# A Flamingo layer on one core: the queries' rms factor moved from q into the exponential, and the transposes of k moved behind the first value matmuls

## What is computed

```
xn = layernorm(x)
q  = rms_norm(xn @ q_w.T + q_b, norm_q_w)          # one rms factor per token, over all 512 features
k  = rms_norm(ctx @ k_img_w.T + k_img_b, norm_k_img_w)
v  = ctx @ v_img_w.T + v_img_b
p  = softmax(q k^T / sqrt(32))                     # per head, 128 x 128
x  = x + tanh(g_xattn) * ((p v) @ o_w.T + o_b)
h  = square(relu(layernorm(x) @ up_w)) @ down_w + (layernorm(x) @ expert_weight) * (sum of the 2 largest gates)
x  = x + tanh(g_ffn) * (layernorm(h) * gamma + beta)
```

## Time and profile before

| | |
|---|---|
| median of 3 runs | 1550.09 us (1548.4 to 1550.29) |
| span of the profiled execution | 1548.3 us; its time outside the profile is not listed apart |
| PE busy | 1499.5 us, 97% of the span |
| VectorE, ScalarE, GpSimd busy | 58%, 45%, 29% |
| attention part | about the first 690 us |
| feed-forward part | the rest |

### The profile page before, as it was taken

The page is one execution under the profiler, slowest core; times in us unless marked ns, Lnnn a source line. Parts: engine busy times, 40 slices in busy tenths (PEclk is TensorE's granted clock), DMA queues, the critical chain, the costliest instruction groups (busy, mean ns, idle before and its releaser), DMA issues.

```text
span 1548.3 us, 22150 instructions
## 1 busy us (share of the span) xinstructions
PE 1499.5 (97%) x6912; PEld 1201.4 (78%) x6912; DVE 892.5 (58%) x1474; ACT 689.9 (45%) x1951; POOL 443.8 (29%) x582
## 2 busy tenths in 40 slices
PE   5999999999999999989999999999999999999996
PEld 4777777777777777767878878878788788788785
DVE  6877777777777777774634334353353343433524
ACT  5667677766676777664422222222222222222221
POOL 3455545444555454440002011020020120200202
PEclk9999999999999999999999999999999999999998
DMA  7222222222222222414310010010100100210100
GB/s 232 62 83 79 68 76 81 70 73 81 81 75 67 81 81 68 123 42 136 109 55 28 1 62 20 14 61 7 54 27 0 54 27 1 67 41 0 41 14 27
DMA packets 76353, 91.75 MB, mean 59 GB/s; under 512 B 7072, under 2 KB 39968, under 8 KB 76320
## 3 DMA queue, kind: packets, MB, share of 16 engines
q1 hardware_dynamic: 76320, 91.34, 19.3%
HBM read 57.76 MB, written 16.78 MB: 48 GB/s over the span
## 4 chain that ended last, share of the span: by engine, by line
PE 78%; DVE 10%; ACT 6%; issue 3%; POOL 1%; DMA 1%; SPq 1%; ACTq 0%; DVEq 0%; POOLq 0%
PE bank L73 14%; PE bank L75 14%; PE bank L74 14%; PE wide L73 10%; PE wide L74 10%; PE wide L75 10%; DVE kf L455 3%; PE bank L270 3%; DVE pT_lo L374 2%; DVE qf L479 2%; ACT pT_hi L537 2%; ACT junk_q L602 1%; ACT junk_k L585 1%; PE bank L824 1%; PE bank L290 1%
## 5 line engine op out<-in xcount | busy, mean ns | idle before, releaser
L1082 ACT ACTIVATE relu<-bank 128x512 f32<-128x512 f32 x128 | 76.7, 599 | 423.6 <-PE bank L75 423.6
L1120 DVE TENSOR_TENSOR hid<-relu 128x512 f32<-128x512 f32 x128 | 97.1, 759 | 269.5 <-ACT relu L1082 269.4
L558 ACT ACTIVATE prob<-wide,nmx 128x128 f32<-128x128 f32 x512 | 180.6, 403 | 39.3 <-DVE nmx L401 39.3
L73 PE MATMUL wide<-down_hi,hT_hi 128*128 128x512 f32 x384 | 152.2, 396 | 0.0
L75 PE MATMUL bank<-wk_hi,up_lo 128*128 128x512 f32 x384 | 152.0, 396 | 0.0
L74 PE MATMUL wide<-down_lo,hT_hi 128*128 128x512 f32 x384 | 151.6, 395 | 0.0
L74 PE MATMUL bank<-wk_lo,up_hi 128*128 128x512 f32 x384 | 151.6, 395 | 0.0
L73 PE MATMUL bank<-wk_hi,up_hi 128*128 128x512 f32 x384 | 151.6, 395 | 0.0
L75 PE MATMUL wide<-down_hi,hT_lo 128*128 128x512 f32 x384 | 151.5, 394 | 0.0
L1122 DVE TENSOR_TENSOR hT_lo<-hid,hT_hi 128x512 fp32r<-128x512 f32 x128 | 89.6, 700 | 89.8 <-ACT hT_hi L1071 89.8
L670 POOL TENSOR_TENSOR prob<-prob,rr 128x512 f32<-128x512 f32 x128 | 137.8, 1087 | 0.0
(11 more groups left out here) (156 smaller groups left out, 3624.7 us busy)
## 6 DMA issues: line engine op xcount, KB each, us to landing
kd<-kT SPq DMA_DIRECT2D x128, 128.0 KB, 2.4
xin<-in_x SPq DMA_DIRECT2D x32, 256.0 KB, 2.7
cin<-in_ctxT SPq DMA_DIRECT2D x32, 256.0 KB, 2.6
xres<-in_x SPq DMA_DIRECT2D x32, 256.0 KB, 2.7
x_scratch<-x SPq DMA_DIRECT2D x32, 256.0 KB, 2.0
fx<-x_scratch SPq DMA_DIRECT2D x32, 256.0 KB, 2.7
fres<-x_scratch SPq DMA_DIRECT2D x32, 256.0 KB, 4.0
out_x<-fres SPq DMA_DIRECT2D x32, 256.0 KB, 2.0
```

The costliest lines, as they stand in the source:

```text
L73: eng.matmul(dst, ah, bh, start=first and k == 0, stop=False)
L558: i = act.activation(prob[:, g, h * P:(h + 1) * P], cols(bank[g], h), ACT.Exp, bias=nmx[:, n:n + 1], scale=1.0, accum_out=rs[:, n:n + 1])
L1082: act.activation(ff.relu[:, :], bank[4 + i % 2], ACT.Relu).then_inc(ff.ac_r, 1)
L1120: dve.tensor_tensor(ff.hid[:, :], ff.relu[:, :], ff.relu[:, :], ALU.mult).then_inc(ff.dv_h, 1)
```

## The change

The raw qb, not qf, is transposed and multiplied with k. The scores are then too large by 1 / rq of their token, which is the partition of the score tile. So the exponential applies rq as its scale (a second operand of 128x1 beside the bias nmx), and the maximum has to be multiplied by rq before it serves as the bias: `maxima` writes raw_mx, and a new `shift` makes nmx = raw_mx * rq, one instruction of 128x4 for each head group, placed one group behind the maxima. qf goes. On PE, V0 now stands ahead of the wait for kf and its transposes.

```diff
@@ tensor
                     if has(a):
                         turn_probs(a, b, 2)
+                        values(a, 0)
                     if has(b):
                         at_least(pe, dv_kf, b + 1)
                         turn(kf, BTK, pe_Tk)
                     if has(a):
-                        values(a, 0)
                         turn_probs(a, b, 3)
...
                     if has(b):
-                        at_least(pe, dv_qf, b + 1)
-                        turn(qf, BTQ, pe_Tq)
+                        at_least(pe, dv_qb, b + 1)
+                        turn(qb, BTQ, pe_Tq)
@@ vector
                     at_least(dve, ac_e, b * NG + (g + 1) - NG)
-                    dve.tensor_reduce(nmx[:, g * HG:(g + 1) * HG], bank[g].rearrange("p (h k) -> p h k", h=HG),
-                                      AX.X, ALU.max, negate=True).then_inc(dv_mx, 1)
+                    at_least(dve, dv_mx, b * NG + (g + 1) - NG)
+                    dve.tensor_reduce(raw_mx[:, g * HG:(g + 1) * HG], bank[g].rearrange("p (h k) -> p h k", h=HG),
+                                      AX.X, ALU.max, negate=True).then_inc(dv_rm, 1)
+
+                def shift(b, g):
+                    gs = slice(g * HG, (g + 1) * HG)
+                    at_least(dve, po_rq, b + 1)
+                    at_least(dve, dv_rm, b * NG + (g + 1))
+                    dve.tensor_scalar(nmx[:, gs], raw_mx[:, gs], rq[:, 0:1], None, ALU.mult).then_inc(dv_mx, 1)
...
-                    if has(b):
-                        at_least(dve, po_rq, b + 1)
-                        dve.tensor_scalar(qf[:, :], qb[:, :], rq[:, 0:1], None, ALU.mult).then_inc(dv_qf, 1)
...
                         for g in range(NG):
                             maxima(b, g)
+                            if g:
+                                shift(b, g - 1)
+                        shift(b, NG - 1)
                         inverse(b, 0)
@@ scalar
                         i = act.activation(prob[:, g, h * P:(h + 1) * P], cols(bank[g], h), ACT.Exp,
-                                           bias=nmx[:, n:n + 1], scale=1.0, accum_out=rs[:, n:n + 1])
+                                           bias=nmx[:, n:n + 1], scale=rq[:, 0:1], accum_out=rs[:, n:n + 1])
```

More of the change, by code:

```diff
@@ L121, in flamingo_layer @@
             nmx = sb(ctx, "nmx", [P, NH])
+            raw_mx = sb(ctx, "raw_mx", [P, NH])
             rs = sb(ctx, "rs", [P, NH])
@@ L135, in flamingo_layer @@
             wh, wl, cst, kdz, kd_in = sem("weights_hi"), sem("weights_lo"), sem("row_consts"), sem("kd_zero"), sem("kd_in")
+            dv_rm = sem("dv_rm")
             pe_K, pe_Q, pe_Tx, pe_TP, pe_PV, pe_Tk, pe_Tq, pe_S, pe_O = (
                 sem("pe_" + n) for n in ("K", "Q", "Tx", "TP", "PV", "Tk", "Tq", "S", "O"))
-            dv_kb, dv_qb, dv_kf, dv_qf, dv_xT, dv_pT, dv_ah, dv_aT, dv_vb, dv_kT, dv_qT, dv_mx, dv_rr, dv_bs, dv_st, dv_xn = (
-                sem("dv_" + n) for n in ("kb", "qb", "kf", "qf", "xT", "pT", "ah", "aT", "vb", "kT", "qT", "mx", "rr", "bs", "st", "xn"))
+            dv_kb, dv_qb, dv_kf, dv_xT, dv_pT, dv_ah, dv_aT, dv_vb, dv_kT, dv_qT, dv_mx, dv_rr, dv_bs, dv_st, dv_xn = (
+                sem("dv_" + n) for n in ("kb", "qb", "kf", "xT", "pT", "ah", "aT", "vb", "kT", "qT", "mx", "rr", "bs", "st", "xn"))
             ac_sk, ac_sq, ac_xT, ac_pT, ac_aT, ac_v, ac_kT, ac_qT, ac_c, ac_e = (
```

## The result

The changed kernel takes 1589.69 us (median of 4, 1588.94 to 1590.6) against 1550.19 before (1548.4 to 1552.78): 1.0253 times as long, with a 95% interval of 1.0239 to 1.0268. That is 39.5 us slower. The direction and the mechanism are those of the forecast; its 28 us were too few, and the time lies only 0.3 us inside the upper end of the range, 1590.

The account below looks back on a forecast made before the run. PE's work plus waits was taken to bound a slot, with 0.24 us spare ahead of TP1. 0.10 + 0.75 + 0.36 - 0.24 = +0.97 us a slot; over 28 slots +27.2, plus 1.2: +28.4, 1578 us, range 1563 to 1590.

Parts of the forecast that it names:

- The bound: Attention slot: PE's work plus its waits; later work from V3 through exponentials and divisions to TP1 counts, except 0.24 us.
- Part 1: V0 ahead of kf's transposes: PE's 0.45 gap closes, but V3 starts 0.10 us later from Q, bounds 0.05 and 0.20.
- Part 2: qf removed: PE's 0.42 us gap closes and VectorE gets 1.42 us back, but nothing on the chain to TP1.
- Part 3: Bias later: first exponential 1.54 us after the first maximum instead of 0.79, +0.75 a slot, between 0.6 and 1.0.
- Part 4: Exponential's second 128x1 operand: 0.09 us each, +0.36 a slot for group 0's four, bounds 0 and 0.4.
- 0 to +0.2 a slot more. I take 0: kf after all 16 exponentials: lands about when PE asks, 4.02 from Q; 0 counted, 0.2 us left for the range.
- the spare time: Ahead of TP1 in a plain slot: 0.24 us of delay absorbed before PE waits for the division, taken from slot 32.
- From slot to total: 28 plain slots at +0.97 give +27.2 us, slot 32 adds 1.2, slots 0 and 1 cancel: +28.4 us.
- Rival A: Exponential's second operand is free, hidden in the overlap with the accumulator read: 0.61 us more a slot, 1568 us; chance 0.16.
- Rival B: Faster: exponentials start no later than the room ahead of TP1 covers, down to -18 us, 1532; chance 0.08.
- Rival C: No difference: added delay near 0.14 to 0.2 us, or first and last slots give back the loss; chance 0.04.
- Rival D: Worse than the sum: kf late by 0.2 as well, shifts at 0.4: +0.4 us a slot, 1589 us; chance 0.10.

Follow-up runs that it names:

- the run with the held division: Changed kernel with GpSimd's division of head group 3 held until VectorE has made kf: 1581.31 us, 1.0205.
- the kernel with the immediate scale: Changed kernel with the exponential's scale an immediate 1.0 and the shift multiplying by ones, rms factor of q left out: 1568.72 us, 1.0129.
- the run with the scale from a tile: Kernel before with the exponential's scale read from a 128x1 tile of ones instead of an immediate: 1568.55 us, 1.0135.

## Why the forecast was right, and where it was short

*The bound.* Right in kind. Both of PE's old gaps closed and the slot grew all the same, because the work that runs from V3 through aT, the bias and the exponentials sets it, and the change makes it longer. The forecast let this work return to PE through the divisions and TP1. In the changed kernel the way back through the end of all 16 exponentials and kf is 0.25 us longer and sets the slot, as the run with the held division shows.

*Part 1.* Right in kind: +0.14 (V3 at 7.20 from Q in the kernel with the immediate scale, 7.06 before), between the ends 0.05 and 0.20 given, where 0.10 was taken. That V0's place loses time by itself was measured twice, at 8 us, and it gained 2.7 us only where kf was late.

*Part 2.* Right: from V3 to the first maximum it is 5.72 us (312.00 to 317.72), 5.70 before (316.69 to 322.39), so nothing is gained on the ring. Taken alone, leaving qf out gains 5 us.

*Part 3.* Right to 0.01: 1.53 us from the first maximum to the first exponential against 1.54 forecast; the shift takes 0.22.

*Part 4.* The first term held: 0.09 for each exponential, 0.36 on the ring. **The step that failed is its last, "0 to +0.2 a slot more. I take 0".** The second operand's cost through the end of all 16 exponentials was 0.25 a slot on V3 (7.45 against 7.20 from Q). The working there had shown that ScalarE's idle 0.77 would be used up, and had named the chain (first copy, square of k, rk, kf); it had kf later by "0.3 or somewhat more" and set that equal to PE's demand without adding the chain up. kf begins 0.52 later from Q (2.70 against 2.18). One error in the working is the 0.36 by which TP1 was to come later "by this part": it was subtracted, but the spare time took it up, and from the first exponential to TP1 it is 6.77 us, 6.75 before (323.18 to 329.93). The 0.25 lies beyond the 0.2 that was left for the range. The run with the held division gives this time back, by a shorter kf.

*The spare time.* Taken as 0.24 from slot 32. In the changed kernel TP1 begins 6.77 us after the first exponential; less the 0.36, that is 6.41, not 6.51, so it was 0.34.

The slot adds up: 0.14 + 0.74 + 0.36 + 0.25 - 0.34 = 1.15, and 0.02 more from TP1 to Q, which needs 0.42 after a wait instead of 0.40, make 1.17; 1.18 to 1.19 were measured. Without the 0.25 of kf it is 0.92, near the forecast 0.97. That is partly luck, since the spare time was taken 0.10 too small and part 1 0.04 too small.

*From slot to total.* PE's first score matmul marks the slots. In slot 1 and slot 31 of the changed kernel:

```profile
53.68 0.50 PE L73 MATMUL wide<-kd,qT_hi 128*128 128x512 f32 x1
...
711.54 0.50 PE L73 MATMUL wide<-kd,qT_hi 128*128 128x512 f32 x1
```

and in the kernel before:

```profile
52.45 0.40 PE L73 MATMUL wide<-kd,qT_hi 128*128 128x512 f32 x1
...
673.90 0.40 PE L73 MATMUL wide<-kd,qT_hi 128*128 128x512 f32 x1
```

The difference grows from 1.23 to 37.64 us: 36.4 over 30 slots, 1.21 each, where I had counted 28 at 0.97, which is 27.2. The slots near the end are not spared (the last of these steps alone grows by 1.7). The first slots bring +1.2, where I had set gain against loss, and from the last scores to the first feed-forward matmul come 2.2 more, where I had 1.2. That matmul in the changed kernel, and in the kernel before:

```profile
731.97 0.47 PE L73 MATMUL bank<-wk_hi,wq_hi 128*128 128x512 f32 x1 [0.81 <-DVE wk_lo L878]
```

```profile
692.13 0.47 PE L73 MATMUL bank<-wk_hi,wq_hi 128*128 128x512 f32 x1 [0.81 <-DVE wk_lo L869]
```

So 39.8 us have gathered there; the feed-forward part takes the same time in both, 856.1 and 856.2 us. Against the forecast 28.4 the slots bring 9.2 too many, the first ones 1.2 and the last 1.0.

*Rival A* (the operand hidden) fell by its own sign, the step between exponentials. *Rival B* (faster) fell at the place it named: TP1 waits for the division. *Rival C* (no difference) fell with the 39.5 us. *Rival D* was half right: kf was late by what it said and a little more, the shifts were not, at 0.22 instead of 0.4. That its 1589 is the measured time is luck: the rest of its sum came from the two slots that were not counted and from both ends. So it is in part luck, too, that the time still lies inside the range.

## What to carry to other kernels

A gap of the busiest engine is worth its length only if the chain behind the next wait has that much room; measure that room where the chain does bind (here a slot at the end), and again at each later waiter, since room at one is not room at the other. An operation that is added sixteen times on an engine with idle time still costs if the first thing queued behind it feeds the bound; add that chain up to the end instead of stopping where the idle time is used up. And before removing an operation because it is late, ask why it takes twice what it takes elsewhere: moving GpSimd's work out of the way of kf and qf kept both operations and won 21 us.

## What the runs showed of the hardware

A VectorE instruction that reads and writes SBUF alone was held up while GpSimd worked on SBUF. qf takes 1.42 us beside GpSimd's addition and 0.48 without; kf takes 1.44 beside its division and 0.74 without. The clearest case is new: with each shift behind its own maximum, the last one of a slot takes 0.90 us instead of the 0.23 of the first (399.07), while GpSimd makes v's low part.

```profile
402.30 0.90 DVE L411 TENSOR_SCALAR nmx<-raw_mx,rq 128x4 f32<-128x4 f32 x1
```

```profile
401.88 1.30 POOL L703 TENSOR_TENSOR v_lo<-vb,v_hi 128x512 fp32r<-128x512 f32 x1 [2.96 <-ACT v_hi L544]
```

The shift ends at 403.20, within 0.02 us of GpSimd's instruction (403.18). By the Trainium skill (SBUF — State Buffer, section Who interferes with whom) the two engines share a pair of ports. VectorE uses it for operations such as `tensor_scalar` in a mode with both ports, and whichever engine issues first then has the pair for its whole instruction while the other stands still. By the same section, a VectorE instruction with two inputs in SBUF contends with a GpSimd instruction that reads SBUF. These rows agree: the `tensor_scalar` of 128x4, whose work is 0.2 us, waited until GpSimd's 128x512 was done. That GpSimd is held up in its turn is not shown here.

A second 128x1 operand costs 0.09 us on an exponential of 128x128 also when the instructions follow each other without a gap: the step with its accumulator read is 0.45 instead of 0.36 at a slot's start. The mean of the listed durations grows a little less, from 403 to 476 ns (the run with the scale from a tile). The overlap between neighbours doesn't hide it.
